# Run 0's queries in two halves of heads, with the null set-up split and the first front and last back part given steps of their own

## Chip, cores and metric

The kernel runs on one core of a Trainium2 chip. The metric is the device time of one execution in microseconds (us). A core has TensorE (PE in the profile, with its weight loads as PEld), VectorE (DVE), ScalarE (ACT), GpSimd (POOL) and SyncE (SP), which only starts DMAs here. Each engine works through its own list of instructions in order, and semaphores tie the lists together.

## What is computed

Nearly all of the work is a six-layer cross-attention model over x (4 sequences of 128 tokens, 128 wide) with a context of 2048 tokens per sequence. A short attention layer and a gated recurrence follow it.

```python
for l in range(L):            # L = 6, H = 16 heads of DH = 64, one key and value head for all
    x = attention(x, None, ..., causal, bias, freqs) + x       # self-attention, 128 keys
    x = attention(x, context, ..., False, None, None) + x      # cross-attention, 2048 keys
    x = feedforward(x, ...) + x
# inside attention: q and k are divided by their norms, a learnt null key and value are put in front,
# softmax(q k^T + bias) v, then @ wo and a layernorm
out = layernorm(x, final_g, stable=True) @ proj_w
```

Self-attention also rotates the first 32 values of each head of q and k (rotary embedding) and adds a bias from a table by distance.

## The kernel before

A **run** is one layer for one of the four sequences: 24 runs (`RUNS`), number n. A run has three parts. Its **front** is the whole self-attention and the making of the cross-attention's queries `QT`, keys `KT` and values `V`. Its **core** is the cross-attention itself: 64 tiles, each 128 keys by 4 heads of 128 queries, after one step for the null key, so 65 steps (`STEPS`). Its **back** is the output projection and the feed-forward part.

A **window** is 65 steps in which the core of run n, the back of run n-1 and the front of run n+1 go on side by side. `drive` writes each engine's list: at each step first that engine's share of the core (`core_step`), then the stages that the tables `PLAN_PE`, `PLAN_ACT`, `PLAN_DVE` and `PLAN_POOL` name for this step. The letter ahead of a stage's name tells its part: `f_` front, `b_` back, `e_` end of a head group of the core, `s_` set-up, `t0_`, `t1_`, `u_`, `v_` the closing layers. The tables fix the order alone; nothing is timed. Window 0 has no core, only the front of run 0 and the set-up. Window 1 has the core of run 0 and the front of run 1, and no back. The last windows carry the closing layers.

In a core step TensorE makes scores in `psS` (three slots), ScalarE takes the exponential twice (`PH`, rounded, and `P`), VectorE subtracts (`PL` = `P` - `PH`, L634), and TensorE, six steps later, adds three products into `psO` (L1097, L1098, L1100).

The front's query preparation, for self-attention (tag `sa`, 17 heads: 16 of q and one of k) and cross-attention (tag `ca`, 16 heads), is a chain over all engines: TensorE projects (`f_proj_sa`, `f_proj_ca`), ScalarE copies to `qraw` (`f_raw_*`), GpSimd rotates (`f_rot`, L452 to L455, `sa` only), ScalarE squares (`f_sq_*`), VectorE sums (`norms`, L568), GpSimd raises to the power -1/2 (`f_sa_q`, `f_ca_q`, L420), VectorE scales (`unit`, L576), ScalarE rounds to 16 bits (`halves`, L891), GpSimd takes the rest (`low`, L461), TensorE transposes (`turn_q`, L1042) and ScalarE copies to `QTs` or `QT` (`queries`, L899).

Set-up on VectorE that window 0 has between the stages of the front: `s_null` (L500 to L517: the null values, constant rows, and the null keys of all layers), `s_table` (L549 the bias table `ET`, then L551 to L554 the null key's bias `b0`, of which the self-attention's null scores, L1056 and L1137, have need), `s_rows` (the input layernorm of sequences 1 to 3, by `layernorm`, L486 to L491). On GpSimd, `s_mask` (L434) masks `ET` once all of it is made. On TensorE, `s_null` transposes the null keys and `s_table` (L1029) makes the table's four blocks.

```python
def head_power(tag, width):
    return lambda n, par: power(rn[:, 0:width], ssc[:, 0:width], width, tag + "_ss", n + 1, tag + "_rn")
```

## Time and profile before

| | us |
|---|---|
| median of 3 runs | 2590.43 |
| lowest, highest | 2587.82, 2591.18 |
| the profiled execution | 2594.97 |
| its span, first to last instruction | 2593.3 |
| PE busy | 2487.2 (96%) |
| DVE busy | 2220.2 (86%) |
| ACT busy | 2057.0 (79%) |
| POOL busy | 604.3 (23%) |

The profile is of one execution, 4.5 us over the median. A row of its timeline gives the start in us from the span's first instruction, the duration, the engine, the source line, the operation with what it writes and reads, and in brackets how long the engine was idle before it and what ended that. TensorE is the engine that is busy nearly throughout, except in window 0 and at the very end.

### The profile page before, as it was taken

The numbers are of one execution on the slowest core, as the hardware profiler recorded it, in microseconds if no ns is written. First come the engines' busy times: TensorE is split into PE (matmuls) and PEld (weight loads), VectorE is DVE, ScalarE is ACT, GpSimd is POOL, SyncE is SP. The second block draws the span as 40 slices with busy tenths as digits, with TensorE's granted clock in tenths as the row PEclk, the third lists the DMA queues.
The fourth block names the chain that finished last, engine by engine and source line by source line (L and its number), as shares of the span: only waits on it lengthen the run. The fifth ranks groups of instructions, "written<-read, shape, count | busy, mean of one in ns | idle before, by whom it ended". The sixth has DMA issues, their size and how long they took to land.

```text
span 2593.3 us, 38049 instructions
## 1 busy us (share of the span) xinstructions
PE 2487.2 (96%) x12652; PEld 1528.1 (59%) x12652; DVE 2220.2 (86%) x4411; ACT 2057.0 (79%) x3973; POOL 604.3 (23%) x392
## 2 busy tenths in 40 slices
PE   4799999999999999999999999999999999999986
PEld 2456656656656566666566566566566565665565
DVE  6689898898898898898898988988988988989874
ACT  2588888888888888888888888888888888888742
POOL 3312312213213213123123122122132131231000
PEclk7799999999999999999999999999999999999985
DMA  3000010001001001001001001001001000000000
GB/s 129 25 9 17 25 35 19 25 8 40 13 13 53 9 17 47 9 17 53 9 17 46 9 17 52 9 17 47 2 24 36 17 25 30 17 9 26 1 1 4
DMA packets 16573, 63.56 MB, mean 25 GB/s; under 512 B 2241, under 2 KB 7410, under 8 KB 11642
## 3 DMA queue, kind: packets, MB, share of 16 engines
q1 hardware_dynamic: 16378, 61.13, 7.3%
q8 instruction: 101, 1.65, 0.3%
q14 instruction: 94, 0.77, 0.1%
HBM read 48.25 MB, written 0.29 MB: 19 GB/s over the span
## 4 chain that ended last, share of the span: by engine, by line
PE 51%; ACT 18%; DVE 17%; issue 10%; POOL 3%; DMA 0%; ACTq 0%; SPq 0%; DVEq 0%; POOLq 0%
PE psS L1049 14%; PE psO L1097 8%; ACT P L884 8%; PE psO L1098 7%; PE psO L1100 7%; ACT PH L881 6%; DVE PL L634 4%; PE psL L1143 3%; PE psL L1154 2%; PE psL L1049 2%; ACT qraw L903 1%; DVE back_x L707 1%; ACT QT L899 1%; POOL back_rstd L420 1%; POOL front_rstd L420 1%
## 5 line engine op out<-in xcount | busy, mean ns | idle before, releaser
L881 ACT ACTIVATE PH<-psS 128x512 fp32r<-128x512 f32 x1536 | 1010.4, 658 | 168.8 <-PE psS L1049 150.1
L634 DVE TENSOR_TENSOR PL<-P,PH 128x512 fp32r<-128x512 f32 x1536 | 1038.6, 712 | 92.9 <-ACT P L884 83.1
L884 ACT ACTIVATE P<-psS 128x512 f32<-128x512 f32 x1536 | 1010.5, 658 | 109.9 <-DVE PL L634 109.8
L1049 PE MATMUL psS<-QT,KT 128*128 128x512 f16 x3072 | 926.6, 383 | 0.8 <-ACT P L884 0.8
L1097 PE MATMUL psO<-PH,V 128*128 128x512 f32 x1536 | 875.5, 570 | 0.0
L1100 PE MATMUL psO<-PL,V 128*128 128x512 f32 x1536 | 606.8, 395 | 0.0
L1098 PE MATMUL psO<-PH,VL 128*64 128x512 f32 x1536 | 605.5, 394 | 0.0
L1049 PEld LDWEIGHTS psS<-QT,KT 128*128 128x128 f16 x3072 | 216.2, 100 | 368.7 <-issue 288.6
L1097 PEld LDWEIGHTS psO<-PH,V 128*128 128x128 f32 x1536 | 291.9, 190 | 177.6 <-ACT PH L881 9.8
L1100 PEld LDWEIGHTS psO<-PL,V 128*128 128x128 f32 x1536 | 288.0, 187 | 151.7 <-DVE PL L634 0.6
L420 POOL TENSOR_TENSOR rn<-ssc,neghalf 128x16 f32<-128x16 f32 (+2 forms) x73 | 240.5, 3294 | 347.7 <-DVE ssc L569 265.9
L420 POOL TENSOR_TENSOR front_rstd<-front_ve,neghalf 128x1 f32<-128x1 f32 x80 | 43.2, 539 | 1012.5 <-DVE front_ve L489 1012.5
L1098 PEld LDWEIGHTS psO<-PH,VL 128*64 128x64 f32 x1536 | 210.2, 137 | 41.0
L461 POOL TENSOR_TENSOR qs_all<-qsq,qs_all 128x1088 f16<-128x1088 f32 (+1 forms) x48 | 114.3, 2381 | 136.8 <-ACT qs_all L891 136.8
L613 DVE STREAM_TRANSPOSE rows_sb<-rcol 64x512 f32<-64x512 f32 x192 | 131.9, 696 | 4.9
L1175 PEld LDWEIGHTS psL<-W,ctx_sb 128*128 128x128 f32 x768 | 101.0, 192 | 12.1 <-issue 2.6
L1143 PE MATMUL psL<-Ps,Vs 128*128 128x512 f32 x192 | 101.4, 610 | 3.5 <-DVE Ps L670 3.5
L1175 PE MATMUL psL<-W,ctx_sb 128*128 128x128 f32 x768 | 101.6, 276 | 0.9 <-ACT kraw L946 0.9
L932 ACT ACTIVATE Ps<-psL 128x512 f32<-128x512 f32 x96 | 66.8, 696 | 38.4 <-PE psL L1049 37.0
L461 POOL TENSOR_TENSOR ks<-ksq,ks 128x1024 f16<-128x1024 f32 x24 | 51.3, 2139 | 171.9 <-ACT ks L956 171.9
L618 DVE TENSOR_TENSOR oTs<-psL,rows_sb 64x256 f32<-64x256 f32 x192 | 80.2, 417 | 6.1
L618 DVE TENSOR_TENSOR oT<-psO,rows_sb 64x256 f32<-64x256 f32 x192 | 80.2, 418 | 6.1
(363 smaller groups left out, 2857.2 us busy)
## 6 DMA issues: line engine op xcount, KB each, us to landing
ctx_sb<-ctxT SPq DMA_DIRECT2D x24, 1024.0 KB, 4.8
KT<-KT SPq DMA_DIRECT2D x48, 256.0 KB, 3.5
W<-wpack SPq DMA_DIRECT2D x6, 1280.0 KB, 5.4
W<-wpack SPq DMA_DIRECT2D x6, 1088.0 KB, 7.3
W<-wpack SPq DMA_DIRECT2D x6, 576.0 KB, 5.7
KT<-biasM SPq DMA_DIRECT2D x1, 1024.0 KB
W<-tail_w SPq DMA_DIRECT2D x1, 832.0 KB
P<-biasW SPq DMA_DIRECT2D x1, 512.0 KB
```

Source lines behind the costliest of these rows:

```text
L420: nc.gpsimd.tensor_tensor(out_, in_, neghalf[0:out_.shape[0], 0:width], ALU.pow).then_inc(sem(done), 1)
L461: nc.gpsimd.tensor_tensor(half, whole, high, ALU.subtract).then_inc(sem(tag + "_lo"), 1)
L618: nc_v.tensor_tensor(dst[64 * odd:64 * odd + 64, 2 * g:2 * g + 2, :], bank[0:64, :].rearrange("p (c a n) -> p c a n", a=2, n=N)[:, :, odd, :],
L634: nc_v.tensor_tensor(PL[:, here, :], P[:, t % PSLOTS, :], PH[:, here, :], ALU.subtract).then_inc(sem("p_lo"), 1)
L881: nc_a.activation(PH[:, t % HSLOTS, :], bank, ACT.Exp, scale=SIM_SCALE).then_inc(sem("p_hi"), 1)
L884: nc_a.activation(P[:, t % PSLOTS, :], bank, ACT.Exp, scale=SIM_SCALE).then_inc(sem("ca_exp"), 1)
L1049: ins = mm(bank, keys[part], q, start=(part == 0), stop=(part == 1))
L1097: mm(bank, V[:, par, j, :], PH[:, here, :], start=False, stop=False)
L1098: mm(bank[0:DH, :], VL[:, par, j, :], PH[:, here, :], start=False, stop=False)
L1100: mm(bank, V[:, par, j, :], PL[:, here, :], start=False, stop=(j == KT_N - 1)).then_inc(sem("ca_pv"), 1)
L1143: mm(psL[:, g % 2, :], Vs[:], Ps[:, g % 2, :], start=True, stop=False)
L1175: ins = mm(psL[:, t % 2, a * 128:(a + 1) * 128], ctx_sb[:, k * 128:(k + 1) * 128], weights(W_CAKV, W_CAKV + 128), start=True, stop=True)
```

## The change

`spans(n, heads)` is new: for run 0 it cuts the heads in two parts, 0 to 7 and 8 to the last, and gives all heads in one part for any other run. `seen` is the count of the semaphore that goes with it. Every stage of the query chain loops over `spans`, so run 0 has two instructions, each with its own wait and its own signal, where the others have one. In window 0 `drive` now calls names that begin with `h_`, which are the front's stages bound to run 0 and have steps of their own. Likewise `l_` names are the back's stages bound to run 23, in the last window but the closing part; their steps are those of the `b_` names.

```diff
+        def spans(n, heads):
+            return ((0, 8), (8, heads)) if n == 0 else ((0, heads),)
+
+        def seen(n, i=1):
+            return i + 1 if n == 0 else n + 2
...
-            0: ["t0_largest", "f_begin", "s_bias", "f_norm_sa", "f_xnT_sa"], 1: ["e_null"], 2: ["s_null"],
+            0: ["t0_largest", "f_begin", "h_begin", "s_bias", "f_norm_sa", "h_norm_sa", "f_xnT_sa", "h_xnT_sa"],
+            1: ["e_null"], 2: ["s_null", "s_values", "s_groups", "s_blank"],
...
-                        part = {"b": back, "f": front, "e": core}[name[0]]
+                        part = {"b": None if tail == "ul" else back, "f": front, "e": core}[name[0]]
...
-            window(None, None, (0, 0), "s")
-            window((0, 0), None, (1, 1))
+            window(None, None, None, "sh")
+            window((0, 0), None, (1, 1), "r")
...
             def head_power(tag, width):
-                return lambda n, par: power(rn[:, 0:width], ssc[:, 0:width], width, tag + "_ss", n + 1, tag + "_rn")
+                def stage(n, par):
+                    for i, (a, b) in enumerate(spans(n, width)):
+                        power(rn[:, a:b], ssc[:, a:b], b - a, tag + "_ss", seen(n, i), tag + "_rn")
+                return stage
...
-                pool.wait_ge(sem("sa_raw"), n * 3 + 3)
+                for k, (a, b) in enumerate(spans(n, 17)):
+                    pool.wait_ge(sem("sa_raw"), 2 + k if n == 0 else n * 3 + 3)
...
+            def low(tag, heads):
+                def stage(n, par):
+                    for i, (a, b) in enumerate(spans(n, heads)):
+                        pool.wait_ge(sem(tag + "_hi"), seen(n, i))
+                        nc.gpsimd.tensor_tensor(qs[:, a:b, 1, :], qn[:, a:b, :], qs[:, a:b, 0, :], ALU.subtract).then_inc(sem(tag + "_lo"), 1)
+                return stage
...
-            def s_null():
+            def s_values():
                 setup(nc_v.tensor_copy(NVH[:], NV))
...
+            def s_groups():
                 setup(nc_v.tensor_reduce(own_group[:], hmask.rearrange("p (g h) -> p g h", h=4), AX_X, ALU.add))
...
+            def s_blank():
                 setup(nc_v.tensor_scalar(B8[:], C[:, 0:QCOL], 0.0, None, ALU.mult))
...
+            def s_null():
                 setup(nc_v.tensor_tensor(nksq, nk, nk, ALU.mult))
...
-                    pe.wait_ge(sem(tag + "_lo"), n + 1)
                     for i in range(2):
+                        pe.wait_ge(sem(tag + "_lo"), seen(n, i))
                         for h in range(8):
```

Four kinds of move come with it.

**Null set-up.** `s_null` now holds the null keys alone and stands first. `s_values` (the null values), `s_groups` and `s_blank` (constants) follow. The null key's bias `b0` leaves `s_table` and becomes `s_b0`, behind the keys' sum of squares. The table's subtractions stand ahead of the queries' scaling, as before. On VectorE from the turned first rows to the transposed null keys, before and after:

```order
L594 TENSOR_SCALAR front_xnT<-psL,gcol 128x128
L500 CAST NVH<-P 128x768
L501 TENSOR_SCALAR P<-P,C 128x768
L502 SCALAR_TENSOR_TENSOR NVH<-NVH,C,P 128x768
L503 TENSOR_REDUCE own_group<-C 128x4
...
L507 TENSOR_SCALAR group_rows<-C 128x128
L508 TENSOR_TENSOR group_rows<-C 8x128
L510 TENSOR_TENSOR rows_sb<-rows_sb 12x64
L511 TENSOR_REDUCE ss<-rows_sb 12x1
L512 TENSOR_SCALAR ssc<-ss 12x1
L514 TENSOR_SCALAR rows_sb<-rows_sb,rn 12x64
```

```order
L644 TENSOR_SCALAR front_xnT<-psL,gcol 128x128
L555 TENSOR_TENSOR rows_sb<-rows_sb 12x64
L556 TENSOR_REDUCE ss<-rows_sb 12x1
L557 TENSOR_SCALAR ssc<-ss 12x1
L559 TENSOR_SCALAR rows_sb<-rows_sb,rn 12x64
L561 CAST nks<-rows_sb 12x64 x2
L562 TENSOR_TENSOR nks<-rows_sb,nks 12x64
L539 CAST NVH<-P 128x768
L540 TENSOR_SCALAR P<-P,C 128x768
L541 SCALAR_TENSOR_TENSOR NVH<-NVH,C,P 128x768
L544 TENSOR_REDUCE own_group<-C 128x4
```

The null keys' six operations moved from behind nine others to the front. On GpSimd, from the null keys' power to the second power of a run, before and after:

```order
L420 TENSOR_TENSOR rn<-ssc,neghalf 12x1
L452 TENSOR_TENSOR qsq<-qraw,C 128x17x16 x2
L453 TENSOR_TENSOR qsq<-qraw,C 128x17x32
L455 TENSOR_TENSOR qraw<-qsq 128x17x32
L420 TENSOR_TENSOR rn<-ssc,neghalf 128x17
L434 AFFINE_SELECT ET<-ET 128x2048
L461 TENSOR_TENSOR qs_all<-qsq,qs_all 128x17x64
L420 TENSOR_TENSOR rn<-ssc,neghalf 128x16
```

```order
L487 TENSOR_TENSOR qsq<-qraw,C 128x8x16 x2
L488 TENSOR_TENSOR qsq<-qraw,C 128x8x32
L490 TENSOR_TENSOR qraw<-qsq 128x8x32
L487 TENSOR_TENSOR qsq<-qraw,C 128x9x16 x2
L488 TENSOR_TENSOR qsq<-qraw,C 128x9x32
L490 TENSOR_TENSOR qraw<-qsq 128x9x32
L449 TENSOR_TENSOR rn<-ssc,neghalf 128x8
L449 TENSOR_TENSOR rn<-ssc,neghalf 128x9
L462 AFFINE_SELECT ET<-ET 128x2048
L496 TENSOR_TENSOR qs_all<-qsq,qs_all 128x8x64
L496 TENSOR_TENSOR qs_all<-qsq,qs_all 128x9x64
L449 TENSOR_TENSOR rn<-ssc,neghalf 128x16
```

Each operation on the queries became two, and the first needs heads 0 to 7 alone.

**Input rows.** `s_rows` becomes `s_row1`, in window 0, and `r_row2` and `r_row3`, which go to steps 60 and 62 of window 1. On VectorE at the end of window 1, before and after (`PL` is the core's subtraction, `oT` the scaled output of a head group, `nv` the null values of the next run, `front_x` the begin of the front in window 2):

```order
L576 TENSOR_TENSOR qsq<-qraw,rn 128x1024
L634 TENSOR_TENSOR PL<-P,PH 128x512 x3
L618 TENSOR_TENSOR oT<-psO,rows_sb 64x256 x2
L634 TENSOR_TENSOR PL<-P,PH 128x512
L659 TENSOR_TENSOR nv<-NVH,own_group 128x4x64
L634 TENSOR_TENSOR PL<-P,PH 128x512 x4
L646 TENSOR_SCALAR front_x<-xs 128x128
```

```order
L626 TENSOR_TENSOR qsq<-qraw,rn 128x1024
L709 TENSOR_TENSOR nv<-NVH,own_group 128x4x64
L684 TENSOR_TENSOR PL<-P,PH 128x512 x3
L668 TENSOR_TENSOR oT<-psO,rows_sb 64x256 x2
L525 BN_STATS front_stats<-eg 128x6
...
L530 TENSOR_SCALAR xs<-eg,front_mv,front_rstd 128x128
L684 TENSOR_TENSOR PL<-P,PH 128x512 x2
L525 BN_STATS front_stats<-eg 128x6
...
L530 TENSOR_SCALAR xs<-eg,front_mv,front_rstd 128x128
L684 TENSOR_TENSOR PL<-P,PH 128x512 x3
L696 TENSOR_SCALAR front_x<-xs 128x128
```

Ten operations of two layernorms stand between the last subtractions of window 1 now, and `nv` stands five places earlier.

**All windows.** In every window `f_nv` moves from step 61 to 57 and `f_KT` from 56 to 55 on VectorE, `e_invert0` and `e_scale0` from 21 and 24 to 24 and 28, `f_kv1` from 6 to 7 on TensorE, and `f_kraw0` from 7 to 8, behind `f_sq_sa`, on ScalarE. GpSimd's order in these windows is as before.

**Steps of window 0 alone.** `h_hi_ca`, `h_turn_q_ca` and `h_QT_ca` stand earlier than their `f_` names (57, 61, 61 for 59, 63, 63). With no core in window 0, this changes nothing in an engine's order there. In the last window the `l_` steps equal the `b_` steps, and SyncE's list is the same throughout.

## Rows read from the trace of the kernel before

**Rows 1.** Stretches: bounds, length, busy us and instructions by engine, PEclk, DMA share, GB/s.

```profile
0.00:96.00 96.00, 44.04 (x155) 23.27 (x159) 55.36 (x140) 22.38 (x33) 28.97 (x30) 0.71 0.28 93
190.00:290.00 100.00, 99.28 (x516) 60.76 (x520) 88.24 (x171) 84.16 (x161) 24.64 (x15) 1.00 0.06 17
```

**Rows 2.** Timeline of window 0, self-attention's queries: start, duration, engine, line, operation.

```profile
17.02 0.35 DVE L594 TENSOR_SCALAR front_xnT<-psL,gcol 128x128 f32<-128x128 f32 x1 [0.57 <-PE psL L1034]
...
20.02 0.60 ACT L903 ACTIVATE qraw<-psL 128x512 f32<-128x512 f32 x1 [1.37 <-PE psL L1109]
...
22.30 0.53 POOL L420 TENSOR_TENSOR rn<-ssc,neghalf 12x1 f32<-12x1 f32 x1 [6.23 <-DVE ssc L512]
22.80 1.69 POOL L452 TENSOR_TENSOR qsq<-qraw,C 128x272 f32<-128x272 f32 x2
22.86 2.96 DVE L514 TENSOR_SCALAR rows_sb<-rows_sb,rn 12x64 f32<-12x64 f32 x1 [0.64 <-POOL rn L420]
24.46 1.31 POOL L453 TENSOR_TENSOR qsq<-qraw,C 128x544 f32<-128x544 f32 x1
...
27.72 3.78 PE L1029 MATMUL psS<-P,C 128*128 128x512 f32 x4
...
33.99 0.69 DVE L549 TENSOR_TENSOR ET<-psO,KT 128x512 f32<-128x512 f32 x1 [0.17 <-PE psO L1029]
...
35.42 2.01 POOL L434 TENSOR_SCALAR_AFFINE_SELECT ET<-ET 128x2048 f32<-128x2048 f32 x1 [1.00 <-ACT ET L860]
35.49 2.21 DVE L553 TENSOR_SCALAR rows_sb<-rows_sb,C 8x512 f32<-8x512 f32 x1
...
39.19 1.28 DVE L576 TENSOR_TENSOR qsq<-qraw,rn 128x1088 f32<-128x1088 f32 x1
...
41.84 2.24 POOL L461 TENSOR_TENSOR qs_all<-qsq,qs_all 128x1088 f16<-128x1088 f32 x1 [4.41 <-ACT qs_all L891]
...
47.36 1.05 PE L1056 MATMUL psL<-QTs,nkcs 128*32 128x512 f16 x8 [0.61 <-ACT QTs L899]
```

**Rows 3.** A stretch of window 0 on VectorE alone: bounds, length, busy us.

```profile
27.40:34.68 7.28, 5.75 (x13) 0.63 0.11 36
```

**Rows 4.** Timeline of window 0, cross-attention's queries, and one input row.

```profile
81.07 0.35 DVE L491 TENSOR_SCALAR xs<-eg,front_mv,front_rstd 128x128 f32<-128x128 f32 x1 [0.65 <-POOL front_rstd L420]
...
82.57 1.06 ACT L927 ACTIVATE qsq<-qraw 128x1024 f32<-128x1024 f32 x1
82.80 0.35 DVE L491 TENSOR_SCALAR xs<-eg,front_mv,front_rstd 128x128 f32<-128x128 f32 x1 [0.65 <-POOL front_rstd L420]
...
85.24 2.91 POOL L420 TENSOR_TENSOR rn<-ssc,neghalf 128x16 f32<-128x16 f32 x1 [2.47 <-DVE ssc L569]
...
90.58 2.12 POOL L461 TENSOR_TENSOR qs_all<-qsq,qs_all 128x1024 f16<-128x1024 f32 x1 [2.43 <-ACT qs_all L891]
```

**Rows 5.** Chain that ended last, end of window 0: start, us, what.

```profile
94.81 1.03 ACT QT L899
...
95.88 1.04 PE psS L1056 x7
```

**Rows 6.** Timeline from the end of window 1 into window 2.

```profile
184.26 2.28 POOL L461 TENSOR_TENSOR qs_all<-qsq,qs_all 128x1024 f16<-128x1024 f32 x1 [2.96 <-ACT qs_all L891]
...
191.02 0.69 DVE L634 TENSOR_TENSOR PL<-P,PH 128x512 fp32r<-128x512 f32 x1 [1.79 <-ACT P L884]
...
193.64 0.33 PE L1034 MATMUL psL<-C,front_xn 128*128 128x128 f32 x1
```

**Rows 7.** Timeline of a later window: its end, then a power on POOL.

```profile
1182.80 2.29 POOL L461 TENSOR_TENSOR qs_all<-qsq,qs_all 128x1024 f16<-128x1024 f32 x1 [2.96 <-ACT qs_all L891]
...
1185.39 1.07 PE L1042 MATMUL psL<-ident,qs_all 128*128 128x128 f16 x16
...
1206.11 3.46 POOL L420 TENSOR_TENSOR rn<-ssc,neghalf 128x17 f32<-128x17 f32 x1 [4.15 <-DVE ssc L569]
...
1207.56 1.29 DVE L634 TENSOR_TENSOR PL<-P,PH 128x512 fp32r<-128x512 f32 x2
```

More of the change, by code:

```diff
@@ L426, in s_null, with in_row @@
                 power(rn[0:12, 0:1], ssc[0:12, 0:1], 1, "null_ss", 1, "null_rn")
-            def s_rows():
-                for b in range(1, B):
-                    power(front.rstd[:], front.ve[:], 1, "in_var", b + 1, "in_rstd")
+            def in_row(b):
+                return lambda: power(front.rstd[:], front.ve[:], 1, "in_var", b + 1, "in_rstd")
             def s_mask():
@@ L457, in low, with f_kv @@
-            def low(tag, half, whole, high):
+                def stage(n, par):
+                    for i, (a, b) in enumerate(spans(n, width)):
+                        power(rn[:, a:b], ssc[:, a:b], b - a, tag + "_ss", seen(n, i), tag + "_rn")
+                return stage
+            def f_kv(n, par):
+                power(rn[:, 0:16], ssc[:, 0:16], 16, "kv_ss", n + 1, "kv_rn")
+            def f_rot(n, par):
+                for k, (a, b) in enumerate(spans(n, 17)):
+                    pool.wait_ge(sem("sa_raw"), 2 + k if n == 0 else n * 3 + 3)
+                    first = qraw[:, a:b, 0:ROT]
+                    pairs = first.rearrange("p h (j t) -> p h j t", t=2)
+                    pb = rotb[:, a:b].rearrange("p h (j t) -> p h j t", t=2)
+                    sinb = sinT.rearrange("p (j t) -> p j t", t=2).unsqueeze(1).broadcast_to([128, b - a, ROT // 2, 2])
+                    for i in range(2):
+                        nc.gpsimd.tensor_tensor(pb[:, :, :, i], pairs[:, :, :, 1 - i], sinb[:, :, :, i], ALU.mult).then_inc(sem("rot_parts"), 1)
+                    nc.gpsimd.tensor_tensor(rota[:, a:b], first, cosT.unsqueeze(1).broadcast_to([128, b - a, ROT]), ALU.mult).then_inc(sem("rot_parts"), 1)
+                    pool.wait_ge(sem("rot_parts"), 3 * seen(n, k))
+                    nc.gpsimd.tensor_tensor(first, rota[:, a:b], rotb[:, a:b], ALU.add).then_inc(sem("sa_rot"), 1)
@@ L538, in s_bias, with in_row @@
                 nc_v.tensor_tensor(ET[0:H, 384:512], ET[0:H, 128:256], ET[0:H, src:src + N], ALU.subtract).then_inc(sem("bias_ready"), 1)
[L541 to L543 removed]
+            def in_row(b):
+                return lambda: setup(layernorm(setup, front, "in", b, x_in[:, b, :], xs[:, b, :]))
             def s_table():
@@ L557, in s_ready @@
                 dve.wait_ge(sem("ET_ready"), 1)
-            links = {}
+            links = {"half": Links(dve, sem("dve_half"), 0)}
             def begin(which, n, per):
+                assert n == 0 or links[which].k == per, links[which].k
                 links[which] = Links(dve, sem("dve_" + which), n * per)
```

115 lines of the change are left out of this document (64 added, 51 removed), and 61 rows, old and new, of tables (PLAN_ACT, PLAN_DVE, PLAN_PE).

## The prediction

> **What bounds the kernel now.** The stretches come first [rows 1]. In a window with a core, TensorE is busy for 99.28 us of 100, at the full clock (PEclk 1.00). Such a window can't get shorter unless TensorE gets less work, and the change gives it the same work. Window 0 is another thing: there TensorE is busy for 44.04 us of 96, no engine is busy for more than 55.36 us, and PEclk is 0.71. It is a chain of short steps that hand over to each other, so there each microsecond taken off the chain counts in full. The timeline of window 0 then shows the chain of the self-attention's queries [rows 2, 3] and that of the cross-attention's [rows 4], which ends with the first null scores of the core at 95.88 [rows 5]. So the gain is to be looked for in window 0, and a loss wherever work is put into windows in which TensorE has nothing to spare.
>
> **Self-attention's queries, window 0.** Before, the chain goes through VectorE: the null set-up from 17.4 (17.02 + 0.35), whose last part is held for 2.96 us, the table on TensorE at once behind it, from 27.72, the last table subtraction at 33.99, then `b0`, of which one operation is held for 2.21 us, and a `V` copy. Only then come the queries' scaling at 39.19, GpSimd's rest at 41.84, and the null scores at 47.36 [rows 2].
>
> What held VectorE: the 12x64 scaling started at 22.86 while GpSimd worked on the rotation (22.80 and 24.46), and took 2.96 us though it has 64 columns. The 8x512 one at 35.49 took 2.21 us beside the mask (35.42 to 37.43). Both read and write SBUF with a single tensor input.
>
> After: the null keys' seven operations, 12 rows by 64 columns, which I put at 0.2 us each from the 0.35 of 128 columns at 17.02, and their power of 0.53 end by 19.5. GpSimd can rotate heads 0 to 7 from 20.6, when ScalarE has copied them (20.02 + 0.60), not from 22.80. Cost of a half: 272 columns take 0.85 (1.69 for two) and 544 take 1.31 [rows 2], so 0.39 + 0.0017 a column. Eight heads are four operations of 128, 128, 256 and 256 columns, 2.9 us; nine heads 3.1. That is 6.0 us for 4.4 in one piece, which only the earlier start pays for.
>
> VectorE now has the constants of `s_groups` and `s_blank` (four scalings, 0.3 to 0.4 us each by the same row) beside this rotation, and these are of the kind that was held. Free of holds they end by 23.6. Held until GpSimd pauses, as at 22.86, they end at 29.5. I take 29.5, as the nearest row is just such a case. The next operations on VectorE (sum of squares, two `V` parts, null copy, four table subtractions) were 5.75 us busy before [rows 3], and the split sum adds two operations, 0.5: the table ends at 35.8, 1.1 later than before (33.99 + 0.69). Unheld, it waits for TensorE's table, which comes a little earlier, and ends at 34.2.
>
> But `b0` and the third `V` part, 4.5 us on VectorE before (34.7 to 39.2), are no longer ahead of the scaling. It starts at 35.8, not 39.19. Both halves take 1.4. The mask (2.0) then runs on GpSimd from 36.6 and the two rests (1.25 and 1.35, from 2.24 for 17 heads) end at 41.2. Second transposes and copy give `QTs` at 43.3. In parallel the fourth key part is copied at 39.4, squares end at 40.4, their sum at 41.8, and the four `b0` operations, 2.1 unheld, at 44.0. The null scores wait for both: 44.05 for 47.36, **3.3 us earlier**. Ends: 4.4 if the constants aren't held, 1.3 if the mask takes its turn ahead of the second scaling and holds it for 2.0. I take **2.8**. From there to the projection for the cross-attention nothing changes in order or length.
>
> Here a statement of the Trainium skill speaks against the change. First the row: GpSimd's power of 17 columns ran from 1206.11 to 1209.57, and two of VectorE's subtractions, with both inputs in SBUF, took 1.29 us for two in the midst of it [rows 7], while the one at 191.02, with GpSimd idle, took 0.69 [rows 6]. So a power does not hold VectorE. The Trainium skill, "SBUF — State Buffer", section "Who interferes with whom", says that a VectorE instruction with two SBUF inputs and a GpSimd instruction that reads SBUF exclude each other for the whole instruction. The trace doesn't bear that out for a power. By that rule `b0` would be held behind the keys' power.
>
> **Cross-attention's queries.** Before: squares from 82.57 (1.06), sum, power from 85.24 (2.91 for 16 columns; one column takes 0.53), scaling (1.28 for 17 heads), rounding, rest 2.12, transposes, `QT` from 94.81 (1.03) [rows 2, 4, 5]. Power costs 0.53 + 0.158 for each further column, so 1.64 for eight. The first squares end at 83.15, their sum with its bound at 84.05, powers at 85.7 and 87.4. The first rest (1.25) then starts at 87.4. If it holds the second scaling, as both read two tensors in SBUF: scaling 88.7 to 89.35, rounding 89.95, rest 91.3, transposes 92.4, copy 93.5, so 2.4 earlier. If the scaling comes first: 92.8, so 3.1. I take **2.7**. ScalarE still makes both squares after both copies, so a part of the overlap isn't there. The keys' copy and swap keep their time, and nothing waited for them before.
>
> **Input rows, windows 1 and 2.** Before, they hid in window 0 under TensorE's projection, so their leaving gains nothing. One takes 1.73 us on VectorE (82.80 less 81.07), 0.65 of it waiting for GpSimd's power [rows 4]. Two put 3.5 us between the last subtractions of window 1. VectorE has 1.79 of idle time there, ahead of the last one at 191.02 [rows 6]. The rest, 1.7, delays `front_x` and with it the turned rows of run 2, for which TensorE starts at 193.64 without any reserve. Queued behind them on VectorE are five subtractions. Besides, `nv` ahead of the subtractions makes the third of them meet GpSimd's rest (184.26, 2.28 long) head on: it is held 1.1 us more than a later one is now. Ends: 1.2 if that subtraction gets its turn first, 2.8 if not. I take **2.6 lost**.
>
> **All later windows.** `nv` (0.4) and the key copy swap places with subtractions, and VectorE's idle time at the window's end covers it (the nearest row is 1.79 in window 1 [rows 6]). `e_invert0` and `e_scale0` free a `psO` bank that is next wanted at tile 32, ten steps later. TensorE's four context products of `f_kv1` go one step later and their user on VectorE is behind anyway. ScalarE's `kraw` copy behind the squares is needed only at step 12. I cost all this at **nothing**, with a bound of 0.2 us a window (below), and gain from none: 0.72 us of idle time is all there is [rows 1].
>
> **Last window.** The `l_` stages have the old steps: nothing.
>
> **Sum.** -2.8 - 2.7 + 2.6 = **-2.9 us**. The profiled execution took 2594.97, so 2592.1 by it. It lies 4.5 above the median of 2590.43, from which the forecast is 2587.5. A measurement of this kernel can tell some 0.2% (5.2 us) from no change; 2.9 is less.
>
> **Rivals.** *Both set-up ends are good and the rows cheap.* 4.4 + 3.1 gained, 1.2 lost: -6.3, 2584.1. For it: GpSimd pauses within its rotation. Against it: the holds of 2.96 and 2.21.
> *Later windows lose.* `nv` shifts the subtractions by 0.34 us against GpSimd's rest. If that subtraction now gets ahead of it, the rest ends 0.34 later than 1185.09 (1182.80 + 2.29), and TensorE's transposes, at 1185.39 [rows 7], lose what goes beyond their reserve. I take half of the 0.30 between the two as hand-over and half as reserve: 0.19 lost. Over 22 windows 4.2 us: -2.9 + 4.2 = +1.3, **2591.7, slower than before**. It decides from 0.15 us of delay. Against it: by my count GpSimd asks first, by less than 0.1 us.
> *A power holds VectorE's `b0`.* Then the null bias comes at 46.5 to 47 and the first 2.8 shrinks to 0.3: 2590.0. Against it: the subtractions of 1.29 for two. The Trainium skill's page on SBUF, named above, has the rule for it.
> *The halves don't overlap*, since each engine serves both in a row and each half pays its fixed cost. Then the cross-attention's chain loses 1 us rather than gain 2.7: +0.8, 2591.2.
> The clock adds to each. PEclk is 0.71 over window 0 and 1.00 later [rows 1], so the core of run 0 starts near the change from 1.2 to 2.4 GHz. When that falls is not known; three microseconds of stretch at the lower level cost half as much, and I allow 1.7 either way.
>
> **Chances.** Forecast 0.50, good ends 0.25, later windows 0.10, power 0.08, no overlap 0.07. With the clock, faster by over 0.2% takes all but a little of the second case and a tail of the first: 0.27. Slower by over 0.2% is the far tail of the third and fourth: 0.05. Within 0.2%: 0.68. The range goes from 2583.0 (good ends and the clock) to 2592.5 (later windows).
>
> **What would show it.** The first null scores of window 0 at 44 (now 47.36), the core's at 90.4 (95.88); VectorE's constants ending near 29.5; powers of 1.6 to 1.8 us; TensorE idle 2 to 3 us ahead of L1034 in window 2; later windows as long as before. Wrong would be: later windows that differ by more than 0.1 us each, or no idle time in window 2.

## The result and the profile after

The changed kernel takes 2581.43 us (median of 8 runs, 2578.42 to 2587.16), the kernel before 2589.73 (median of 8, 2587.82 to 2593.08). The ratio is 0.9968, with a 95% interval of 0.9957 to 0.9979: 8.3 us less, between 5.4 and 11.1. The forecast was 2587.5, with 2583.0 as its lower end, and "within 0.2%" as the likeliest case. It moved by 0.32%. The direction of the sum was right and its size was not: the measured median lies below the forecast's lower end.

The profiled execution of the changed kernel took 2580.11 us (span 2578.4), that of the kernel before 2594.97. These 14.9 us are more than the medians show. What a kernel's profile says is therefore read below as times of places in the program, from two profiles of each kernel (`b_again` and `a_again` are the kernel before and the changed one, once more):

| us from the start | before | `b_again` | changed | `a_again` |
|---|---|---|---|---|
| null scores of window 0 | 47.36 | 46.31 | 40.77 | 40.68 |
| TensorE starts the cross-attention's projection | 78.12 | 74.61 | 71.92 | 71.34 |
| from its end to the first core's start | 13.97 | 13.98 | 11.24 | 11.24 |
| first core's start | 95.88 | 92.37 | 86.94 | 85.97 |
| first to second core's start | 94.11 | 93.83 | 93.13 | 94.02 |
| second to third | 99.88 | 99.87 | 100.78 | 100.80 |
| third to last core's start, 21 windows, mean | 99.87 | 99.91 | 99.85 | 99.86 |
| last core's start | 2387.06 | 2384.22 | 2377.67 | 2377.90 |
| from there to VectorE's last instruction | 204.06 | 199.51 | 198.18 | 197.24 |

Up to the last core's start the two pairs differ by 6.3 to 9.4 us, and on average by 7.9, close to the 8.3 of the medians. What comes behind it is nearly the same code in both kernels (two stages of the core stand a few steps later), and in the fifteen runs below it took from 197.1 to 205.3, with no order by kernel. The first two profiles happened to have 204.06 and 198.18 there.

Stretches of the changed kernel, to be held against [rows 1] (columns: stretch, its length, busy us and instructions of TensorE, its weight loads, VectorE, ScalarE, GpSimd; granted clock; DMA share; GB/s):

```profile
0.00:96.00 96.00, 49.58 (x191) 25.47 (x192) 55.65 (x142) 30.69 (x54) 33.28 (x39) 0.77 0.28 93
...
190.00:290.00 100.00, 99.37 (x514) 60.93 (x513) 88.52 (x171) 83.98 (x161) 25.07 (x16) 1.00 0.05 17
1088.00:1188.00 100.00, 99.37 (x515) 60.95 (x514) 88.67 (x172) 83.99 (x160) 25.07 (x16) 1.00 0.11 34
```

A window with a core is as full as before. Window 0 holds more of TensorE's work in its first 96 us, since the core begins in them.

The timeline of its window 0 (columns: start us, us, engine, line, operation, out<-in), against [rows 2]:

```profile
20.77 1.92 POOL L487 TENSOR_TENSOR qsq<-qraw,C 128x128 f32<-128x128 f32 x2 [2.19 <-ACT qraw L954]
...
22.64 0.77 POOL L488 TENSOR_TENSOR qsq<-qraw,C 128x256 f32<-128x256 f32 x1
22.86 0.83 DVE L549 TENSOR_SCALAR B<-C 128x512 fp32r<-128x512 f32 x1
23.49 0.78 POOL L490 TENSOR_TENSOR qraw<-qsq 128x256 f32<-128x256 f32 x1
23.73 0.63 DVE L550 TENSOR_SCALAR group_rows<-C 128x128 fp32r<-128x128 f32 x1
24.23 1.10 POOL L487 TENSOR_TENSOR qsq<-qraw,C 128x144 f32<-128x144 f32 x2
24.39 0.53 DVE L551 TENSOR_TENSOR group_rows<-C 8x128 fp32r<-8x128 f32 x1
...
27.55 1.88 PE L1082 MATMUL psO<-QT,C 128*128 128x512 f32 x4
...
31.43 1.28 DVE L593 TENSOR_TENSOR ET<-psO,KT 128x512 f32<-128x512 f32 x2
...
32.62 1.35 DVE L626 TENSOR_TENSOR qsq<-qraw,rn 128x512 f32<-128x512 f32 x2
...
35.81 2.61 POOL L496 TENSOR_TENSOR qs_all<-qsq,qs_all 128x512 f16<-128x512 f32 x2
35.91 1.37 DVE L702 TENSOR_TENSOR nvs<-NVH,own_group 128x256 fp32r<-128x256 f32 x1
...
38.70 3.00 POOL L449 TENSOR_TENSOR rn<-ssc,neghalf 128x16 f32<-128x16 f32 x1 [0.28 <-DVE ssc L742]
...
39.42 0.47 DVE L600 TENSOR_SCALAR rows_sb<-rows_sb,C 8x512 f32<-8x512 f32 x1
...
40.77 1.04 PE L1109 MATMUL psL<-QTs,nkcs 128*32 128x512 f16 x8 [1.04 <-DVE B L601]
```

In the kernel before, the first two of these constants and `nvs` took:

```profile
20.56 0.43 DVE L506 TENSOR_SCALAR B<-C 128x512 fp32r<-128x512 f32 x1
21.02 0.23 DVE L507 TENSOR_SCALAR group_rows<-C 128x128 fp32r<-128x128 f32 x1
...
40.59 0.42 DVE L652 TENSOR_TENSOR nvs<-NVH,own_group 128x256 fp32r<-128x256 f32 x1
```

The constants (L546 to L551) meet the rotation and are slowed, 0.83 us where the kernel before has 0.43 and 0.63 where it has 0.23, but each gets in at the next border between two of GpSimd's operations (these start at 22.64, 23.49 and 24.23). They end at 24.9, not at 29.5. TensorE's table ends at 29.4 and VectorE's at 32.7, where the scaling starts. `b0` ends as the last thing before the null scores, 0.1 us behind `QTs`, and the keys' power (38.70 to 41.70) doesn't hold it. What is held on its way is `nvs`, the null values of the self-attention: 1.37 us beside GpSimd's first rest, 0.42 in the kernel before, with GpSimd idle.

The cross-attention's queries, same view, against [rows 4, 5]:

```profile
76.23 1.14 ACT L980 ACTIVATE qsq<-qraw 128x512 f32<-128x512 f32 x2
...
77.92 3.25 POOL L449 TENSOR_TENSOR rn<-ssc,neghalf 128x8 f32<-128x8 f32 x2 [4.83 <-DVE ssc L618]
...
81.15 1.14 POOL L496 TENSOR_TENSOR qs_all<-qsq,qs_all 128x512 f16<-128x512 f32 x1
81.20 1.64 DVE L626 TENSOR_TENSOR qsq<-qraw,rn 128x512 f32<-128x512 f32 x1 [0.92 <-POOL rn L449]
...
86.94 1.04 PE L1109 MATMUL psS<-QT,nkc 128*32 128x512 f16 x8 [1.11 <-ACT QT L950]
```

The second scaling starts 0.05 us behind GpSimd's first rest and is held by it (1.64 for 0.69), as the lower of the two ends of that term had it.

And the end of window 1 with the two input rows in it, GpSimd, VectorE and TensorE:

```profile
174.34 2.62 POOL L496 TENSOR_TENSOR qs_all<-qsq,qs_all 128x1024 f16<-128x1024 f32 x1 [2.95 <-ACT qs_all L942]
```
```profile
173.07 1.89 DVE L684 TENSOR_TENSOR PL<-P,PH 128x512 fp32r<-128x512 f32 x3
```
```profile
184.64 0.33 PE L1087 MATMUL psL<-C,front_xn 128*128 128x128 f32 x1 [0.77 <-DVE front_xn L530]
```

The third subtraction behind `nv` started at 174.27, 0.07 us ahead of GpSimd's rest, and wasn't held; the rest took 2.62 instead of 2.28. TensorE then waits 0.77 for `front_xn`, not 2 to 3.

### The profile page after: what moved, and what is told of

Same layout as the page of the kernel before. It is cut to its first block, busy times and chain, and to the rows that moved or that the text cites. A ratio compares the mean times of both kernels' runs of the same rounds, so it can differ in the third digit from the quotient of the medians.

```text
span 2578.4 us, 38069 instructions
## 1 busy us (share of the span) xinstructions
PE 2478.3 (96%) x12652; PEld 1524.9 (59%) x12652; DVE 2221.3 (86%) x4417; ACT 2053.2 (80%) x3977; POOL 615.2 (24%) x400
## 4 chain that ended last, share of the span: by engine, by line
PE 71%; DVE 17%; issue 5%; ACT 5%; POOL 2%; DMA 0%; SPq 0%; DVEq 0%; POOLq 0%; ACTq 0%
PE psS L1102 20%; PE psO L1150 11%; PE psO L1151 11%; PE psO L1153 11%; DVE PL L684 6%; PE psL L1196 3%; ACT P L934 2%; PE psL L1207 2%; PE psL L1102 2%; ACT PH L931 2%; PE psL L1214 2%; DVE V L734 1%; DVE back_x L756 1%; POOL back_rstd L449 1%; PE psL L1095 1%
## 5 line engine op out<-in xcount | busy, mean ns | idle before, releaser
L931 ACT ACTIVATE PH<-psS 128x512 fp32r<-128x512 f32 x1536 | 1031.7, 672 | 180.4 <-PE psS L1102 160.6
L934 ACT ACTIVATE P<-psS 128x512 f32<-128x512 f32 x1536 | 1037.9, 676 | 109.8 <-DVE PL L684 109.6
L449 POOL TENSOR_TENSOR rn<-ssc,neghalf 128x16 f32<-128x16 f32 (+4 forms) x75 | 240.8, 3211 | 341.0 <-DVE ssc L618 264.1
L496 POOL TENSOR_TENSOR qs_all<-qsq,qs_all 128x1088 f16<-128x1088 f32 (+3 forms) x50 | 122.6, 2453 | 131.4 <-ACT qs_all L942 131.4
```

Of the source, the lines that this page charges most:

```text
L449: nc.gpsimd.tensor_tensor(out_, in_, neghalf[0:out_.shape[0], 0:width], ALU.pow).then_inc(sem(done), 1)
L931: nc_a.activation(PH[:, t % HSLOTS, :], bank, ACT.Exp, scale=SIM_SCALE).then_inc(sem("p_hi"), 1)
L934: nc_a.activation(P[:, t % PSLOTS, :], bank, ACT.Exp, scale=SIM_SCALE).then_inc(sem("ca_exp"), 1)
```

## The experiments

The theory after the result: the order of the null set-up and of `b0`, the halves of the self-attention and those of the cross-attention are three parts that add, and the forecast went wrong where it had GpSimd hold VectorE's constants. Rivals: the halves made all of it; the clock made it; the later windows gave some.

All results in one table ("null": start of the null scores of window 0; "projection to core": as above; "window 2": second to third core's start). A ratio is to the kernel before as timed beside that kernel, on the same chip. The chips differ by up to 2.5 us in the median of the kernel before, so medians of different rows are compared by their ratios:

| kernel | null | projection to core | first core | window 2 | median us | ratio to before |
|---|---|---|---|---|---|---|
| `a_whole` | 42.80 | 13.96 | 91.35 | 104.50 | 2591.09 | 0.9996 (0.9987 to 1.0005) |
| `a_whole2` | 42.71 | 13.97 | 90.72 | 104.50 | one run, 2590.78 | |
| `a_sa_only` | 40.62 | 13.97 | 89.89 | 100.81 | 2586.63 | 0.9982 (0.9972 to 0.9992) |
| `a_ca_only` | 42.87 | 11.26 | 88.18 | 100.80 | one run, 2584.29 | |
| `b_null_order` | 42.99 | 13.98 | 89.69 | 99.86 | 2585.98 | 0.9980 (0.9971 to 0.9988) |
| `a_null_last` | 41.77 | 11.24 | 85.23 | 100.78 | one run, 2579.80 | |
| `a_b0_early` | 42.93 | 11.24 | 88.77 | 100.80 | one run, 2589.54 | |
| `a_blank8` | 43.17 | 11.25 | 88.71 | 100.81 | one run, 2582.96 | |
| `a_whole_small3` | 42.57 | 13.97 | 91.78 | 100.80 | one run, 2585.46 | |
| `a_rows_back` | 40.76 | 11.27 | 86.21 | 99.89 | 2576.77 | 0.9955 (0.9940 to 0.9969) |
| `a_rows_back2` | 40.65 | 11.35 | 87.21 | 99.91 | 2579.91 | 0.9959 (0.9946 to 0.9971) |
| `a_old_late` | 40.36 | 11.24 | 86.90 | 100.76 | 2580.66 | 0.9961 (0.9946 to 0.9976) |
| `a_fill` | 40.46 | 11.29 | 83.95 | 99.92 | 2578.59 | 0.9958 (0.9943 to 0.9973) |
| `a_again` | 40.68 | 11.24 | 85.97 | 100.80 | 2581.20 | 0.9963 (0.9951 to 0.9976) |
| `b_again` | 46.31 | 13.98 | 92.37 | 99.87 | one run, 2587.57 | |

**No halves.** `a_whole` is the changed kernel with

```diff
         def spans(n, heads):
-            return ((0, 8), (8, heads)) if n == 0 else ((0, heads),)
+            return ((0, heads),)
```

and its waits counted to match.

> The changed kernel with no halves: the queries of run 0 are prepared in one piece, in self-attention and in cross-attention; the changed order of the null set-up, of b0 and of the input rows stays. Theory (the order made most of the gain of the first 40 us, since VectorE's constants get through between GpSimd's rotation operations): the rotation runs from 22.4 to 26.8, the constants are delayed by one GpSimd operation each at most and end by 26, the null scores of window 0 start at 41.0 to 42.0 (40.77 with halves, 47.36 in the kernel before), and the core starts at 90.0 to 90.5, since the cross-attention's halves are worth 2.7. Rival (the halves made the gain): null scores at 44 or later, core at 92 or later. Total: 3 us slower than the changed kernel by the theory, 5 to 7 by the rival.

Null scores at 42.80, and in `a_whole2`, the same kernel once more, at 42.71. That is 0.8 beyond the range of the theory (41.0 to 42.0) and short of the rival's 44; the core came at 91.35, 0.9 beyond the theory's range. What the theory had left out is `nvs` again, on VectorE ahead of `b0`. GpSimd, VectorE and TensorE:

```profile
36.76 2.28 POOL L499 TENSOR_TENSOR qs_all<-qsq,qs_all 128x1088 f16<-128x1088 f32 x1
```
```profile
36.85 2.46 DVE L705 TENSOR_TENSOR nvs<-NVH,own_group 128x256 fp32r<-128x256 f32 x1
```
```profile
42.80 1.05 PE L1112 MATMUL psL<-QTs,nkcs 128*32 128x512 f16 x8 [1.10 <-DVE B L604]
```

So the order alone, without any halves, brings 3.5 to 4.6 of the 5.5 to 6.6 us, and the self-attention's halves 2.0. Of these, 0.9 come from the earlier start of `nvs` (35.91 for 36.85), and 1.1 from its shorter hold beside a rest of half the length (1.37 for 2.46).

But the total was that of the kernel before: by the ratios 7 us behind the changed kernel, where the theory had 3. The place that the theory didn't have is window 2, 104.5 long for 100.8. VectorE, GpSimd and TensorE there:

```profile
178.76 3.83 DVE L687 TENSOR_TENSOR PL<-P,PH 128x512 fp32r<-128x512 f32 x3
```
```profile
179.68 2.37 POOL L499 TENSOR_TENSOR qs_all<-qsq,qs_all 128x1024 f16<-128x1024 f32 x1 [3.36 <-ACT qs_all L945]
```
```profile
192.03 0.33 PE L1090 MATMUL psL<-C,front_xn 128*128 128x128 f32 x1 [2.84 <-DVE front_xn L533]
192.20 1.02 PE L1105 MATMUL psS<-QT,KT 128*128 128x512 f16 x2
```

Here the rest began at 179.68, 0.29 us ahead of the third subtraction (179.97), which then took 2.63 us instead of 0.68. TensorE waited 2.84 us, and its next pairs of scores took 1.02 us for 0.60. The Trainium skill, "SBUF — State Buffer", section "Who interferes with whom", says that issue order decides who blocks whom, and, of VectorE's two-port modes, that the one that comes first keeps the shared pair for its whole instruction. Here both engines read two tensors. The order of the starts decides in these rows too: 0.07 us behind, the rest took 0.34 more, and 0.29 behind, the subtraction took 1.95 more. The 0.34 is less than the 0.61 for which the subtraction still ran, so that case isn't a hold to the end by these rows.

> The changed kernel with no halves, once more. Theory (which of VectorE's subtraction and GpSimd's rest gets its turn first in window 1 is a race that falls anew): the three subtractions behind nv take 1.9 this time and the next window 100.8, or 3.8 and 104.5 again; in the first case the execution takes 2586 to 2588, in the second 2590 or more. Null scores at 42.6 to 42.9 in either. Rival (the cost belongs to this kernel): 104.5 again, which one repetition would leave possible.

It was 3.83 and 104.50 again. So in two profiles of this kernel it wasn't drawn anew; that it belongs to the phase of this kernel fits this, but two profiles don't show it. `a_whole_small3`, which has no halves either but three small operations more in window 0, has 1.89 there and 100.80. In all the profiles with `nv` ahead of the subtractions it is one or the other: 2.6 us for the third subtraction in `a_whole` twice, 0.7 in the rest.

**One half each.** In `a_sa_only` only spans of 17 heads are split, in `a_ca_only` only those of 16.

> The changed kernel with halves in self-attention alone; the cross-attention's queries of run 0 go in one piece. Theory: nothing moves up to the null scores (40.77), and the core starts 2.7 later than with both (86.94), at 89.6. Rival (halves of the cross-attention don't overlap, and the stretch before the core got shorter by the clock): the core starts at 87.5 or earlier.

> The changed kernel with halves in the cross-attention alone. Theory (order, self-attention's halves and cross-attention's halves are three parts that add): null scores at 42.6 to 42.8 as with no halves, and 11.24 us from the end of TensorE's cross-attention projection to the core, as with both. Rival (the halves help only together): more than 12.5.

From the projection's end to the core it is 13.97 without and 11.26 with the cross-attention's halves; the null scores are at 40.62 and 42.87. The two sorts of halves act apart, and add. (42.87 is 0.07 beyond the expected range.)

**The order alone, on the kernel before.** `s_null` goes first on VectorE, the rest of the old one behind it in three stages, and `b0` to its own stage:

```diff
-            0: [...], 1: ["e_null"], 2: ["s_null"],
+            0: [...], 1: ["e_null"], 2: ["s_null", "s_values", "s_groups", "s_blank"],
...
+            17: ["s_b0"],
```

> The kernel before with one edit: on VectorE the null keys' set-up goes first, the values, groups and blanks behind it, and the null bias row b0 goes to step 17 behind the keys' sums. No halves, the rest as before. Theory (order): null scores of window 0 at 41.5 to 42.5 for 47.36, core start at 90.4 to 91.0 for 95.88, total 5 us less than before. Rival (holds come back, as the rotation is in one piece here and began at 22.80 before): the constants end at 26 to 27, null scores at 44, total 3 us less. Rival (the gain was of the clock): null scores at 46 or later, unless TensorE's table runs at the full clock.

Null scores at 42.99, and 5.8 us less by the median. That is 0.5 beyond the range, since GpSimd's mask held the scaling (from 33.03, 3.06 us instead of 1.28). The core starts at 89.69, 0.7 ahead of the range. The stretch from the null scores to the projection took 28.95 us there, for 30.76 in the kernel before, and this is the stretch that the clock moves (below). Window 2 keeps its 99.86, as no rows were moved into window 1.

**Which part of the order.** `a_null_last` puts `s_null` behind the constants again, `a_b0_early` puts `s_b0` right behind `s_table`; both keep the halves.

> The changed kernel with the null keys' set-up behind the constants again, as in the kernel before; the halves stay. GpSimd's power of the null keys then ends at 22.8 and the rotation of the first half starts there: two operations of 0.6, one of 0.8, a pause, one of 0.8. Theory (a scaling that asks right behind the start of the rotation is held to GpSimd's next pause, not to the next border): it takes 2.0 us, to 24.9. Rival (it gets in at the first border): 0.6. Null scores at 42.0 to 42.6 for 40.77, core start 1.3 to 1.8 later than the changed kernel.

> The changed kernel with b0's four operations back behind the table, ahead of the queries' scaling. Theory (b0's place is the larger half of the order's gain): the third of them meets GpSimd's mask at 33.5 and is held by it to 35.5, the scaling starts at 36.2 for 32.62, and the null scores at 43.5 to 44.4 for 40.77. Rival (its place is worth nothing, since the null scores wait for b0 in either order): 41.5 or earlier.

The null keys' place is worth 1.0 us (41.77 for 40.77), below the expected range (42.0 to 42.6), and the core start can't show it: it came at 85.23, as the stretch ahead of it had more of the full clock. `b0`'s is worth 2.2 (42.93), also less than expected (43.5 to 44.4). The scaling does start 3.8 later, but the null scores no longer wait for `b0` then, they wait for `QTs`. VectorE and GpSimd in `a_b0_early`:

```profile
33.47 2.21 DVE L632 TENSOR_SCALAR rows_sb<-rows_sb,C 8x512 f32<-8x512 f32 x1
35.71 0.74 DVE L633 SCALAR_TENSOR_TENSOR B<-B,C,rows_sb 8x512 fp32r<-8x512 f32 x1
36.38 1.34 DVE L658 TENSOR_TENSOR qsq<-qraw,rn 128x512 f32<-128x512 f32 x2
```
```profile
33.40 2.01 POOL L494 TENSOR_SCALAR_AFFINE_SELECT ET<-ET 128x2048 f32<-128x2048 f32 x1 [2.90 <-ACT ET L942]
```

It is the hold of 2.21 of [rows 2] once more, by the mask. So null keys 1.0, `b0` 2.2 and halves 2.0 make 5.2, for 5.5 between `b_again` and the changed kernel.

**What a real hold would have cost.** `a_blank8` makes the 128x512 blank eight times:

```diff
-                setup(nc_v.tensor_scalar(B8[:], C[:, 0:QCOL], 0.0, None, ALU.mult))
+                for again in range(8):
+                    setup(nc_v.tensor_scalar(B8[:], C[:, 0:QCOL], 0.0, None, ALU.mult))
```

> The changed kernel with the 128x512 blank of VectorE's constants made eight times in place of once, at 22.9: three or four of them meet GpSimd's rotation and take 0.8 each, the others 0.43, so that the constants end near 29 and not at 24.9. Theory (the forecast's arithmetic was right and only its hold of the constants to 29.5 wrong): the table ends at 35.3, the queries' first scaling starts there, and the null scores start at 43.6 to 44.2 for 40.77. Rival (another step, TensorE's table or the halves, carried the 3.3 us): null scores at 42 or earlier.

```profile
22.82 5.87 DVE L550 TENSOR_SCALAR B<-C 128x512 fp32r<-128x512 f32 x8
28.72 0.23 DVE L551 TENSOR_SCALAR group_rows<-C 128x128 fp32r<-128x128 f32 x1
28.98 0.28 DVE L552 TENSOR_TENSOR group_rows<-C 8x128 fp32r<-8x128 f32 x1
...
35.02 1.35 DVE L627 TENSOR_TENSOR qsq<-qraw,rn 128x512 f32<-128x512 f32 x2
```

The constants end at 29.26, nearly where the forecast had them, the scaling starts at 35.02 (forecast 35.8), and the null scores at 43.17. That is 2.4 later than with constants that end at 24.9. The hold that I put in was worth 2.4 of the 3.3 us between the forecast null scores (44.05) and the measured ones. The expected 43.6 to 44.2 was missed by 0.4: the operations between the constants and the scaling take 5.76, where I had 6.25. The theory expected the scaling at 35.3 and it started at 35.02; the rival's 42 or earlier is out.

**The hold from which I sized the step.**

> The kernel before once more, unaltered. Theory (the hold of 2.96 us of the 12x64 scaling was one outcome of a race with GpSimd's rotation, which started 0.06 us ahead): it may get in at a border this time and take 0.9 or 1.7, and the null scores then start 1 to 2 earlier than 47.36; with the same outcome all repeats to 0.3. Rival (it is no race): 2.96 and 47.36 again, which one repetition can't exclude. The stretch from the end of the cross-attention's projection to the core takes 13.97 in either.

> The changed kernel without halves, with three more scalings of 12x64 by rn (into a scratch, in the form of the one that took 2.96 us in the kernel before) on VectorE at 22.5, just as GpSimd has begun its rotation in one piece (two of 0.85, one of 1.31, a pause, one of 1.35). Theory (a scaling gets in at the next border between GpSimd's operations): the three end near 23.2, 24.2 and 25.5, and the constants behind them at 27. Rival (such a small one is held to GpSimd's pause at 25.5, as in the kernel before): the first takes 3 us.

VectorE in `b_again`, in `a_whole_small3` and in `a_null_last`, in this order:

```profile
22.67 2.95 DVE L514 TENSOR_SCALAR rows_sb<-rows_sb,rn 12x64 f32<-12x64 f32 x1 [0.64 <-POOL rn L420]
```
```profile
22.09 2.87 DVE L553 TENSOR_SCALAR rows_sb<-rows_sb,rn 12x64 f32<-12x64 f32 x3
```
```profile
22.88 0.50 DVE L592 TENSOR_SCALAR rows_sb<-rows_sb,rn 12x64 f32<-12x64 f32 x1 [0.64 <-POOL rn L482]
23.42 1.31 DVE L594 CAST nks<-rows_sb 12x64 f16<-12x64 f32 x2
```

The hold of 2.96 [rows 2] came again, 2.95, past two borders of GpSimd's rotation. The null scores came 1.05 earlier all the same (46.31), since the table's last subtraction ended at 33.63 for 34.68; so "the same outcome" did not repeat to 0.3. Three scalings of that form beside the same rotation took 2.87 together: each got in at the next border. The very same instruction beside a rotation in halves took 0.50, not the 2.0 of that run's theory; the cast behind it, though (from 23.42, the first of two that take 1.31 together in the row of that kernel), was passed over at one border (23.8) and got in at the pause at 24.5. So being passed over is real, the same in both profiles of the kernel before, and not the rule. What decides it was not found: 0.06 us behind the start of GpSimd's operation the scaling was passed over in the one kernel and not in the other.

**The changed kernel again.**

> The changed kernel once more, unaltered, to see what varies from one execution to the next. Theory: up to the second core's start and in windows 3 to 22 it repeats itself to 0.3 us; the window from the second core's start is either 100.8 again or, where the third subtraction behind nv is held by GpSimd's rest this time, 102 to 104.5; what is left of the spread of 9 us between runs lies in the last core window and the tail, at the lower clock. Rival: the first 90 us vary by several us themselves.

Null scores to 0.1, window 2 to 0.02, windows 3 to 22 to 0.02. The core starts 1.0 earlier than in the first profile, so the first 90 us vary more than the 0.3 expected; it lies between the null scores and the projection (30.66 for 31.15) and in the projection (3.39 for 3.78), and window 1 gives 0.9 of it back. The rest of the spread is in the tail, as expected.

**Input rows.** `a_rows_back` puts `r_row2` and `r_row3` behind `s_row1` in window 0.

> The changed kernel with the input rows of samples 2 and 3 back in window 0, where the kernel before had them. Theory: the window from the second core's start gets back from 100.78 to 99.9, and the 0.77 of idle TensorE ahead of L1087 at its start goes. In window 0 the rows stand ahead of the cross-attention's first sum, which comes earlier than before; they take 3.5 us of VectorE from about 73: nothing lost there if the projection isn't done by then, up to 2 if it is. Total: between 0.9 faster and 1 slower than the changed kernel.

> The changed kernel with the input rows of samples 2 and 3 in window 0, once more, on the same chip as the changed kernel itself. Theory: 1.4 us less than the changed kernel up to the third core's start (0.7 in window 0, 0.9 in the window behind), and by the median 1 to 3 us less, 0.05 to 0.1 per cent. Rival (its lower median of 2576.77 was a matter of how many runs fell on the shorter tail): no difference of the medians beyond 1 us.

Window 2 is 99.89 and 99.91, so the rows cost 0.9 there. In window 0 they run on VectorE from 71.0 to 76.2, under TensorE's projection (to 74.9) and ScalarE's first squares (to 76.1), so that the first sum comes just behind them at 76.22: from the projection to the core it takes 11.27 and 11.35 for 11.24. The medians are 2576.77 and 2579.91, for 2581.20 of the changed kernel timed beside the second; the intervals overlap nearly wholly. By window 2 it is 0.9 better, by the median it can't be told from the changed kernel. The 1.4 us less up to the third core's start, which were expected of `a_rows_back2`, didn't come: 281.24 for 280.85 and 280.79 in the two profiles of the changed kernel (`a_rows_back` had 279.34).

**Later windows.** `a_old_late` undoes the moves there.

> The changed kernel with the moves in later windows undone: nv, the key copy, the inversion and scaling of the first context bank, the kv context product and the kraw copy stand where the kernel before had them; window 0 keeps its halves. Theory (the moves are worth nothing): windows 3 to 22 at 99.85 each as in both kernels. The window from the second core's start gets to 100.8 or less, since nv is behind the subtractions again. Rival (the moves bring 0.1 us a window, which the first windows' gain hid): 99.95 or more each, 2 us in all.

99.87 a window on average, 0.01 to 0.02 from the others, and window 2 at 100.76. The moves are worth nothing that this can tell, and `nv`'s place costs nothing where the subtraction goes first.

**The clock.** `a_fill` adds products that nobody reads to `a_rows_back`, where TensorE waits in window 0 of run 0:

```diff
+            def fill(count):
+                for again in range(count):
+                    mm(psO[:, 1, :], group_rows[:], B8[:], start=True, stop=True)
...
+                if tag == "ca" and n == 0:
+                    fill(5)
                 pe.wait_ge(sem(tag + "_xn"), n + 1)
```

> The changed kernel with the input rows of samples 2 and 3 in window 0, and with fourteen products of 128x512 that nobody reads on TensorE in its idle stretches of window 0: three ahead of the self-attention's out projection (58.7 to 61.8), five ahead of the turned rows (65.6 to 70.2), five and one ahead of the turned queries (76.5 to 84). They sit where TensorE waits, and cost at most 0.5 us of overshoot each time. Theory (the clock is worth microseconds here: it is at half for most of 48 to 90, and TensorE was mostly idle ahead of these stretches): the projection takes 1.9 instead of 3.78, the core starts at 83 to 84 instead of 86.2 to 87.2, and the window from there takes 93.1 or less. Rival (the clock doesn't rise by that): core start at 86 to 88.

The core starts at 83.95, 2.3 and 3.3 earlier than in `a_rows_back` and `a_rows_back2`, within the theory's range. But the projection itself still takes 3.78, where the theory had 1.9, and the window from the core's start takes 93.35, not 93.1 or less. By the median (2578.59) no difference from `a_rows_back2` can be told. From the null scores to the projection, about the same stretch of the program, in the kernel before, in `b_again`, in the changed kernel, in `a_fill` and in `a_null_last` (third number from the end: granted clock):

```profile
47.00:78.00 31.00, 18.34 (x46) 7.90 (x46) 17.97 (x42) 4.53 (x8) 3.98 (x4) 0.56 0.00 1
```
```profile
46.00:75.00 29.00, 15.01 (x47) 7.06 (x48) 18.35 (x44) 4.48 (x8) 3.94 (x4) 0.79 0.00 1
```
```profile
41.00:72.00 31.00, 18.14 (x47) 7.93 (x39) 18.07 (x41) 4.31 (x7) 3.93 (x4) 0.61 0.00 1
```
```profile
40.00:69.00 29.00, 16.94 (x55) 8.53 (x55) 18.68 (x43) 4.58 (x8) 4.63 (x4) 0.79 0.00 1
```
```profile
42.00:71.00 29.00, 15.25 (x47) 7.06 (x40) 18.47 (x44) 4.31 (x7) 4.08 (x5) 0.79 0.00 1
```

At 0.56 and 0.61 TensorE needs 18.3 and 18.1 us for its work and the stretch is 30.8 and 31.2 long; at 0.79 it needs 15.0, and the stretch is 28.3. The clock moves this stretch by 2.5 us in one and the same kernel (the kernel before and `b_again`). And `b_again` and `a_null_last` have 0.79 and 28.3 to 28.4 us there without any product that nobody reads, `a_fill` has 28.4 with them. So it isn't shown that the added products brought the core forward; the clock of that stretch differs as much without them.

Nor did the clock make the gain of the change. In `b_again` VectorE waits for TensorE's table by less than 0.2 us, and the null scores are still 5.5 later than in the changed kernel; and from the projection to the core the kernels have 13.96 to 13.98 without the cross-attention's halves and 11.24 to 11.35 with them, in every profile.

## Why the prediction was wrong, point by point

The change brought 5.4 us more than the forecast. Two terms were mis-sized: the self-attention's queries by 2.7 (against `b_again`), and the input rows by 1.7. The remaining 1.0 isn't placed and lies within the interval.

*What bounds the kernel.* Right. Windows with a core kept their 99.85 us, and everything was won in window 0.

*Self-attention's queries, forecast 2.8, measured 6.6 (5.5 against `b_again`).* This is the step that failed. "I take 29.5, as the nearest row is just such a case": the constants ended at 24.9, since each got in at the next border between GpSimd's operations. `a_blank8` puts 2.4 us on it. The row doesn't give 29.5 either: its scaling ended at 25.82, within the rotation (to 27.22), in a gap of 0.08 us ahead of GpSimd's last operation, and the working from there to 29.5 isn't told. The nearest row was a single one. It repeats in `b_again`, and a cast in `a_null_last` was passed over too, but the three scalings in `a_whole_small3`, the one in `a_null_last` and the constants of the changed kernel were not. The instruction was of another size and place in the queue than the constants, and I had no second row of a hold past a border. A second cause: the unheld end, 4.4, was too small itself. It had VectorE wait for TensorE's table until 34.2 (1.6 ahead of the held case, which from 3.3 would make 4.9 and not 4.4). In the changed kernel VectorE didn't wait for the table at all and ended it at 32.71, and neither did it in `b_null_order`, where TensorE's table ended only at 31.3. A third: 1.05 us lie in the kernel before, whose table had the lower clock in its first profile (ended at 34.68, in `b_again` at 33.63).

*Halves there.* I had them pay only by the earlier start. They are worth 2.0, and 1.1 of it is the shorter hold of `nvs` ahead of `b0`, which the forecast had free of holds. That the null scores wait for `b0` last was right. The shape was right: powers 1.66 and 1.80 (forecast 1.6 to 1.8), the two rests 2.61 (2.60).

*Cross-attention's queries, forecast 2.7, measured 2.73* (13.97 to 11.24), with the second scaling held by the first rest (1.64). By the forecast's own working that case was the end of 2.4, 0.3 less than came; 2.7 was a value between its two ends, and its hitting the measured one to 0.03 is in part luck.

*Input rows, forecast 2.6 lost, measured 0.9.* Both cases of that term have been seen: 0.77 of idle where the subtraction gets its turn first, and 2.84 (with 4.6 us on the window, since the clock fell too) where the rest does. I took the second; in the changed kernel it is the first. So this term was on the wrong side of a decision of some 0.35 us, which I couldn't read from the order. Its good end was too dear as well: 1.2, and by its own terms (2.8 less 1.1) 1.7, for 0.9.

*Later windows, forecast nothing.* Right: 99.85 each. Only one window differed, the one before the last core, 100.17 in the profile before; `b_again` has one of 100.26 in the same place, so it isn't of the change.

*The rivals.* What came was the first rival, both ends good and the rows cheap (-6.3), to which I gave 0.25. With measured terms it is -5.5 - 2.7 + 0.9 = -7.3, for a median of -8.3; the remaining 1.0 lies within the interval. A power that holds `b0`: no. Its operations took 0.41, 0.47 and 0.74 beside the power; the last of them, the only one with two tensor inputs, took the same 0.74 in the kernel before with GpSimd idle. Halves that don't overlap: no. Later windows lose: no.

*The clock, allowed 1.7 either way.* Too little for one profile: 2.5 us before the projection, and up to 8 from the last core's start to the end. From 2482 us on the granted clock was 0.66 in `a_rows_back` (205.3 us) and 0.74 in the changed kernel (198.2). The medians even that out in part. With 1.7 the range would have begun at 2582.4 (2584.1 less 1.7), not at 2583.0, and the measured median of 2581.43 lies below either.

## What to carry to other kernels

Before a hold is put into a sum from its longest row, look at all the rows where the two engines meet: here most waiting operations got in at the next border between the other's instructions, and a few were passed over. Where an instruction of VectorE and one of GpSimd that hold each other start within 0.4 us, forecast both outcomes as separate cases, since the price isn't a mean of them. And in a start-up chain the place in the queue can pay as much as a split: moving the four operations of `b0` out from in front of the self-attention's queries gave 2.2 us, cutting these queries in halves 2.0.

## What the runs showed of the hardware that I had not expected

A full window doesn't forgive a pause. In `a_whole` TensorE stood still for 2.84 us in a stretch at full clock, and the clock fell to half behind it: 0.57 over the next 4 us, then full again. Window 2 is 104.50 long there, 3.7 more than in the changed kernel, for 1.95 us of a held subtraction: 2.1 are the longer pause, the other 1.6 come with the lower clock. `a_whole2` has the same pause and the same fall. Pauses of 0.8 us at the same place, in the changed kernel and eight others, left the clock at 1.00.

```profile
192.00:196.00 4.00, 3.97 (x10) 2.47 (x11) 2.21 (x4) 0.34 (x2) 0.00 (x0) 0.57 0.00 0
196.00:200.00 4.00, 4.00 (x21) 2.54 (x20) 1.31 (x2) 3.76 (x8) 1.62 (x2) 1.00 0.01 2
```
